# Attention: values of two key blocks and the denominators in one array visit, three banks for transposed scores, maxima placed by DMA, compact reciprocals

## The reference

```
q, k_s, v_s, k_l, v_l = heads of x@Wq, x@Wkv_short, x@Wkv_long      # 16 heads of 32
out_short = softmax(q k_s^T / sqrt(32) - |i-j|(1-decay)) v_s
out_long  = softmax(q k_l^T / sqrt(32)) v_l
out = (alpha*out_short + (1-alpha)*out_long) @ Wo
```

## Time and profile before

| | |
|---|---|
| time, median of 3 runs | 5613.65 us (5612.13 to 5614.03) |
| profiled execution, first to last instruction | 5613.5 us |
| of it attention, from the first maximum to the last mix | 641.8 to 4278.9 us |
| busy: TensorE, weight load, VectorE, ScalarE, GpSimd | 96%, 38%, 74%, 51%, 52% |
| mean granted TensorE clock | 0.981 |

### The profile page before, as it was taken

One profiled execution on the slowest core, in us unless ns is written; L12 is line 12 of the kernel. 1 busy time (PEld: TensorE's weight loads), 2 busy tenths in 40 slices (PEclk: granted clock), 3 DMA queues, 4 the chain that ended last, 5 costly groups with the idle time before them and its releaser, 6 DMA issues. The chain is left out here.

```text
span 5613.5 us, 97704 instructions
## 1 busy us (share of the span) xinstructions
PE 5382.8 (96%) x28780; PEld 2121.9 (38%) x28780; DVE 4180.9 (74%) x7218; ACT 2874.8 (51%) x5201; POOL 2933.2 (52%) x658
## 2 busy tenths in 40 slices
PE   7999899999999999999999999999996999999999
PEld 3444333333322323223233332232332555555555
DVE  5444688877877878778778787787883777777777
ACT  1111166666666666666666666666664333333332
POOL 0000088878877878778778787788884000000000
PEclk9999799999999999999999999999998999999999
DMA  4333201010101010101010101010101000000000
GB/s 135 105 104 93 81 19 33 21 29 22 33 21 29 21 34 21 29 21 33 22 29 21 34 21 29 21 33 22 29 3 49 17 22 17 22 17 22 17 22 12
DMA packets 145632, 191.62 MB, mean 34 GB/s; under 512 B 18500, under 2 KB 97988, under 8 KB 145030
## 3 DMA queue, kind: packets, MB, share of 16 engines
q1 hardware_dynamic: 145159, 185.65, 11.2%
HBM read 123.56 MB, written 61.64 MB: 33 GB/s over the span
## 5 line engine op out<-in xcount | busy, mean ns | idle before, releaser
L764 DVE TENSOR_REDUCE rowmax_parts<-scores_qk 128x1 f32<-128x512 f32 x4096 | 2569.8, 682 | 668.9 <-PE scores_qk L836 666.3
L745 ACT ACTIVATE probs_T<-scores_kq 128x512 f32<-128x512 f32 x4096 | 2263.3, 596 | 1249.5 <-PE scores_kq L836 1195.2
L704 POOL TENSOR_TENSOR probs_group_sum<-probs_T 128x2048 f32<-128x2048 f32 x384 | 1742.4, 4538 | 667.4 <-PE sums L913 395.7
L836 PE MATMUL scores_kq<-q_operand,k_operand 103*128 103x512 f16 (+3 forms) x3712 | 1279.8, 351 | 16.7 <-ACT probs_T L745 15.4
L704 POOL TENSOR_TENSOR probs_group_sum<-probs_group_sum,probs_T 128x2048 f32<-128x2048 f32 x256 | 1185.5, 4631 | 46.0 <-POOL probs_group_sum L704 45.1
L836 PE MATMUL scores_qk<-k_operand,q_operand 96*128 96x512 f16 (+4 forms) x3712 | 1178.9, 354 | 22.8 <-DMA k_operand<-positions_dram 18.5
L903 PE MATMUL outputs_T<-probs_T,v_operand 128*32 128x512 f32 x8192 | 1103.3, 611 | 52.4 <-issue 52.4
L836 PEld LDWEIGHTS scores_qk<-k_operand,q_operand 96*128 96x128 f16 (+1 forms) x3712 | 352.7, 98 | 898.6 <-DVE rowmax_parts L764 627.1
L1341 PE MATMUL f_gate_up<-w_gate_up,xq_T 128*128 128x352 f32 x2048 | 626.4, 462 | 0.8 <-issue 0.8
L836 PEld LDWEIGHTS scores_kq<-q_operand,k_operand 103*128 103x128 f16 x3712 | 361.2, 98 | 672.9 <-ACT probs_T L745 507.1
L1341 PEld LDWEIGHTS f_gate_up<-w_gate_up,xq_T 128*128 128x128 f32 x2048 | 382.5, 190 | 200.7 <-issue 2.6
(11 more groups left out here) (144 smaller groups left out, 3477.2 us busy)
## 6 DMA issues: line engine op xcount, KB each, us to landing
qk_parts_dram<-qk_parts SPq DMA_DIRECT2D x96, 256.0 KB, 2.5
q_operand<-qk_parts_dram SPq DMA_DIRECT2D x192, 128.0 KB, 2.6
k_operand<-qk_parts_dram SPq DMA_DIRECT2D x192, 128.0 KB, 2.9
v_dram<-v_heads SPq DMA_DIRECT2D x16, 1024.0 KB, 5.4
v_operand<-v_dram SPq DMA_DIRECT2D x64, 256.0 KB, 3.1
q_operand_above<-qk_parts_dram SPq DMA_DIRECT2D x96, 128.0 KB, 2.8
x_groups<-x SPq DMA_DIRECT2D x8, 1024.0 KB, 8.8
attention_dram<-o_mixed SPq DMA_DIRECT2D x128, 64.0 KB, 1.6
```

The costliest lines, as they stand in the source:

```text
L704: nc.gpsimd.tensor_tensor(total, first, probs[:, b % PBUF, :], ALU.add).then_inc(added.sem, 1)
L745: nc.scalar.activation(probs[:, kb % PBUF, qt * BANK:(qt + 1) * BANK], pb[:, k % 2, :], ACT.Exp)\
L764: nc.vector.reduce_max(rowmax[:, w % 2, c // NQ, c % NQ:c % NQ + 1], pa[:, k % 3, :], AX.X)\
L836: return nc.tensor.matmul(out, lhsT, rhs, start=start, stop=stop, skip_group_check=True)
```

## The change

TensorE's order is now in 8 steps a unit. A step has a burst (`times_v` of two key blocks, then the `count`s due at this step) and 8 slots, each with one transposed score chunk and one chunk for maxima. Transposed scores run 11 chunks ahead of the burst instead of 6 or so and have three banks (the bank that the transposes used is free). Maxima of a later unit are 20 chunks ahead instead of 16. VectorE's order follows the slots: `take` before slot 56, `invert` 16, `weigh` 32, `mix` 36; `negate` falls after slot 43's chunk.

Maxima are written as float16 into a 128 x 32 tile, turned by VectorE in 32 x 32 blocks, and put into the operand's row by four DMAs for each operand (8 in even units, 4 in odd ones). The denominators are gathered by four DMAs from one partition of 512 columns into 32 partitions of 16, inverted as one 128 x 16 reciprocal, written to DRAM by one DMA and read back by four, each spread over 32 partitions.

```diff
-ASTEPS = 12
-TURN_MAX = 12
-INVERT = 3
-WEIGH = 8
-MIX = 10
+BURST = 2
+STEPS = KB // BURST
+SLOTS = BURST * NQ
+LEAD = SLOTS + 3
+EARLY = 20
+TAKE_SUMS = 5
+INVERT = 16
+WEIGH = 32
+MIX = 36
+TAKE = (STEPS - 1) * SLOTS
-COUNT_LAG = 3
+COUNT_AT = (2, 4, 5, 7, 8, 9)
+def maximum_of(g):
+    c = (g + EARLY) % CHUNKS
+    return (1 if g + EARLY < CHUNKS else 2), c
...
-        negmax = sb("negmax", [P, 2, KB], F32)
-        maxT = sb("negmax_T", [KB, 2, P], F16)
+        negmax = sb("negmax", [P, 2, HD], F16)
+        maxT = sb("negmax_T", [P, 2, HD], F16)
+        sums_c = sb("sums_compact", [P, KB], F32)
+        inv_c = sb("inverse_compact", [P, KB], F32)
-        pb = ps("scores_kq", [P, 2, BANK], F32)
+        pb = ps("scores_kq", [P, 3, BANK], F32)
-        pt = ps("turned", [P, BANK], F32)
...
             def place_max(w, n):
-                sp.wait_ge(roundm.sem, roundm.at(n, w + 1))
+                sp.wait_ge(turned.sem, turned.at(n, w + 1))
                 for dst in (q_op[w], q_up[w]) if w % 2 == 0 else (q_op[w],):
-                    sp.dma_start(dst[MROW:MROW + 1, :], maxT[:, w % 2, :]).then_inc(maxrow[w].sem, 16)
+                    row = dst[MROW:MROW + 1, :].rearrange("o (c g j) -> o c g j", g=NQ, j=HD)
+                    for g in range(NQ):
+                        sp.dma_start(row[:, :, g, :], maxT[g * HD:g * HD + KB, w % 2, :]).then_inc(maxrow[w].sem, 16)
+            def gather_sums(w, n):
+                wait_apart(sp, sums_out, sums_out.at(n, w + 1), passed)
+                wait_apart(sp, inverted, inverted.at(n, w), passed)
+                for qt in range(NQ):
+                    sp.dma_start(sums_c[qt * HD:(qt + 1) * HD, :], sums[qt * HD:qt * HD + 1, :].rearrange("o (r e) -> o r e", e=KB))\
+                        .then_inc(gathered.sem, 16)
+            def spread_inverse(w, n):
+                wait_apart(sp, inverted, inverted.at(n, w + 1), passed)
+                sp.dma_start(inv_scr[w % 2:w % 2 + 1, :].rearrange("o (p e) -> (o p) e", e=KB), inv_c[:, :])\
+                    .then_inc(inv_out.sem, 16)
+                wait_apart(sp, inv_out, inv_out.at(n, w + 1), passed)
+                wait_apart(sp, weighed, weighed.at(n, w), passed)
+                for qt in range(NQ):
+                    sp.dma_start(inv[qt * HD:(qt + 1) * HD, :],
+                                 inv_scr[w % 2:w % 2 + 1, qt * BANK:(qt + 1) * BANK].to_broadcast([HD, BANK]))\
+                        .then_inc(inv_in.sem, 16)
...
                 for w in range(UNITS):
+                    back = unit_before(w, n, first)
+                    if back:
+                        gather_sums(*back)
+                        spread_inverse(*back)
+                        if back[0] % 2:
+                            store(back[0] // 2, back[1])
                     if after(w, n, last):
                         place_max(*after(w, n, last))
-                    if w == 0 and not first:
-                        store(1, n - 1)
-                    if w == 2:
-                        store(0, n)
...
-            def round_max(w, n):
...
             def take_sums(w, n):
                 act.wait_ge(counted.sem, counted.at(n, (w + 1) * GROUPS_N))
-                act.wait_ge(weighed.sem, weighed.at(n, w))
+                act.wait_ge(gathered.sem, gathered.at(n, w * NQ))
...
             def negate(w, n):
                 dve.wait_ge(maxed.sem, maxed.at(n, (w + 1) * (CHUNKS + 1) - 1))
-                nc.vector.tensor_reduce(negmax[:, w % 2, :], rowmax[:, w % 2, :, :], AX.X, ALU.max, negate=True)\
+                nc.vector.tensor_reduce(negmax[:, w % 2, 0:KB], rowmax[:, w % 2, :, :], AX.X, ALU.max, negate=True)\
                     .then_inc(maxed.sem, 1)
+                dve.wait_ge(maxed.sem, maxed.at(n, (w + 1) * (CHUNKS + 1)))
...
+                nc.vector.transpose(maxT[:, w % 2, :], negmax[:, w % 2, :]).then_inc(turned.sem, 1)
...
-            def invert(w, n, r):
-                dve.wait_ge(sums_out.sem, sums_out.at(n, w + 1))
-                nc.vector.reciprocal(inv[:, r * P:(r + 1) * P], sums[:, r * P:(r + 1) * P]).then_inc(inverted.sem, 1)
+            def invert(w, n):
+                dve.wait_ge(gathered.sem, gathered.at(n, (w + 1) * NQ))
+                dve.wait_ge(inv_out.sem, inv_out.at(n, w))
+                nc.vector.reciprocal(inv_c[:, :], sums_c[:, :]).then_inc(inverted.sem, 1)
...
+                    for g in range(CHUNKS):
+                        if g == TAKE:
                             take(w, n)
+                        if back and g == INVERT:
+                            invert(*back)
+                        if back and g == WEIGH:
                             weigh(*back)
+                        if back and g == MIX and back[0] % 2:
+                            mix(back[0] // 2, back[1])
+                        distance, c = maximum_of(g)
                         unit = after(w, n, last, distance)
+                        if unit:
                             max_chunk(*unit, c)
                             if c == CHUNKS - 1:
                                 negate(*unit)
...
-            def turn_max(w, n):
...
+                    pe.wait_ge(expd.sem, expd.at(n, number - 2))
-                bank = pb[:, number % 2, :]
+                bank = pb[:, number % 3, :]
...
+                    for j in range(STEPS):
+                        for kb in range(BURST * j, BURST * (j + 1)):
+                            times_v(w, n, kb)
+                        for u, behind in (((w, n), 0), (back, STEPS)):
+                            for g in range(GROUPS_N):
+                                if u and COUNT_AT[g] == j + behind:
+                                    count(*u, g)
+                        for s in range(SLOTS):
+                            b = j * SLOTS + s + LEAD
+                            if b < CHUNKS:
+                                scores_for_exp(w, n, b)
+                            elif ahead:
+                                scores_for_exp(*ahead, b - CHUNKS)
+                            distance, c = maximum_of(j * SLOTS + s)
+                            unit = after(w, n, last, distance)
                             if unit:
+                                scores_for_max(*unit, c)
```

More of the change, by code:

```diff
@@ L529, in adds_until, with last_with @@
     return sum(max(0, sum(b <= max(kb, g[1]) for b in g) - 1) for g in GROUPS if g[0] <= kb)
-def chunks_of(i):
-    k = (i - ASTEPS) % KB * NQ
-    return (1 if i < ASTEPS else 2), list(range(k, k + NQ))
-EARLY = (KB - ASTEPS) * NQ
+def maximum_of(g):
+    c = (g + EARLY) % CHUNKS
+    return (1 if g + EARLY < CHUNKS else 2), c
+def last_with(k, ring, total):
+    return max(m for m in range(total) if m % ring == k)
 ROW_LOADS = UNITS + 6 * UNITS // 2
@@ L731, in one_pass @@
                     for kb in range(KB):
-                        if back and kb == COUNT_LAG + 1:
+                        if back and kb == TAKE_SUMS:
                             take_sums(*back)
-                        if kb == (TURN_MAX + 2) % KB and after(w, n, last):
-                            round_max(*after(w, n, last))
                         old = w * KB + kb - PBUF
@@ L755, in _ @@
         def _(dve):
+            nc.vector.memset(negmax[:, :, :], 0.0)
             for w in (1, 3):
@@ L802, in one_pass @@
                 for w in range(UNITS):
-                    ahead, back = after(w, n, last), unit_before(w, n, first)
-                    for i in range(KB):
-                        if i == KB - 1:
+                    back = unit_before(w, n, first)
+                    for g in range(CHUNKS):
+                        if g == TAKE:
                             take(w, n)
-                        if back and INVERT <= i < INVERT + NQ:
-                            invert(*back, i - INVERT)
-                        if back and i == WEIGH:
+                        if back and g == INVERT:
+                            invert(*back)
+                        if back and g == WEIGH:
                             weigh(*back)
-                        distance, chunks = chunks_of(i)
+                        if back and g == MIX and back[0] % 2:
+                            mix(back[0] // 2, back[1])
+                        distance, c = maximum_of(g)
                         unit = after(w, n, last, distance)
-                        for c in chunks if unit else ():
+                        if unit:
                             max_chunk(*unit, c)
@@ L816, in one_pass @@
                                 negate(*unit)
-                        if back and i == MIX and back[0] % 2:
-                            mix(back[0] // 2, back[1])
             one_pass(0, True, False)
@@ L824, in _ @@
             end = (UNITS - 1, PASSES - 1)
-            for r in range(NQ):
-                invert(*end, r)
+            invert(*end)
             weigh(*end)
@@ L928, in one_pass @@
                     ahead, back = after(w, n, last), unit_before(w, n, first)
```

(32 more changed lines are left out.)

60 lines of the change are left out of this document (33 added, 27 removed).

## The result

| | before | after |
|---|---|---|
| median, same chip | 5613.42 us (4 runs) | 5851.66 us (4 runs, the lowest 5850.01) |
| profiled execution, first to last instruction | 5613.5 us | 5850.6 us |
| mean granted TensorE clock | 0.981 | 0.968 |

The ratio is 1.0424, with a 95% interval of 1.0407 to 1.0441: 238 us slower. The forecast was slower by 115 us (5728), with a range that ended at 5786. One of the four runs after took 7741.39 us at a granted clock of 0.647; the ratio leaves it out, and the other three lie between 5850.01 and 5852.63.

A forecast was written before the change was run, and what follows sets the result against it. TensorE was held by the ring of three score banks, waiting for VectorE's maxima. A pass of 231.4 us against 224.0, over some 15.5 passes, gave +115, ends +3: 5731, stated as 5728 us, range 5562 to 5786.

The forecast's parts named there:

- The stretch between bursts is 16 score matmuls with the same three banks for maxima: Between bursts, VectorE's chain of reductions sets the pace: 4.09 us a stretch, 32.7 a unit against 32.4 before.
- the forecast's plain unit: A unit summed without contention: 54.5 us against 54.4 before, including 0.35 for the mix of every second unit.
- they miss: Second rival: weighing and mix miss GpSimd's adds, other terms as taken; 5607 us, no measurable change, chance 0.15.
- the collision: Two-input VectorE steps (weighing, mix) block until GpSimd's running add ends; 8.0 us a pass in all.
- price of 1.7: The weighing, asked for in the middle of the sixth add, delays the reductions by 1.7 us a unit.
- The first rival: Weighing and mix miss the adds and the bursts gain: a pass of 220.6, 5563 us, chance 0.26.
- Price 1.7 in every second unit: The mix, asked for during the seventh add, takes 2.4 us instead of 0.7.
- escapes: After a boundary, the weighing is asked for near the sixth add's end and costs nothing; the mix pays some 1.2.
- the boundary, 5.4: Pass boundary: 5.4 us instead of 6.4, as full banks and a burst cover the 1.0 ScalarE's pause costs TensorE.
- late maxima, 0.15 a unit: In even units the eighth maxima DMA lands 0.6 us late; the ring swallows most, leaving 0.15 on average.
- the third rival: Maxima land 2.3 us late as well: 58 us more, 5786, chance 0.12; sign: their waits not under 20 us.
- the end: After the loop, gathering and spreading the sums in place of four reciprocals: +6 us.

The follow-up runs named there:

- e9: e1 with each of VectorE's maxima taken over 256 of the 512 columns of a bank: 5438.88 us, ratio 0.9678.
- e10: e6 with each of VectorE's maxima taken over 256 of the 512 columns of a bank: 5492.76 us, ratio 0.9777.
- e1: The changed kernel with weighing and mix both moved to slot 56, and maxima ahead of the store on SP's queue: 5612.05 us, ratio 0.9995.
- e2: e1 with the weighing back at slot 32, so only the mix is at slot 56: 5721.36 us, ratio 1.0190.
- e7: e1 with the maxima of a later unit 24 chunks ahead instead of 20: 5563.34 us, ratio 0.9911.
- e6: The changed kernel with visits of one key block instead of bursts of two, and weighing and mix at slot 56: 5514.13 us, ratio 0.9822.

## Why the prediction was wrong, point by point

**Right: what bounds the new order.** "The stretch between bursts is 16 score matmuls with the same three banks for maxima": 4.09 forecast, 4.10 to 4.16 measured; bursts 1.88 and 2.76 against 1.86 and 2.71. e9 and e10 show the cause and not only the number: with a faster VectorE the stretches between bursts fall, and those of single visits stay. The sum is less sound than it looks. In e1 the mix is off the path, so the forecast's plain unit is 54.5-0.35 = 54.15 there; 54.39 and 53.99 were measured. But e1's nearness to 5607 ("they miss", 5 us) is in part luck: with the mix hidden, 22 us less, the forecast is 5585, and most of the 27 us that it is short by is the boundary.

**Right: that the collision decides, and where it lies.** The phases are those of the forecast (1.51 and 2.91 us into the sixth and seventh add, forecast 1.4 and 2.9), and the weighing takes 3.6 us instead of 0.75. Its price of 1.7 fits as a mean (1.71); a pass pays 7.0 for weighings and not 5.1. The first rival (missed, 5563), the second (5607) and their 0.41 fell with the two rows of o_weighed.

**Wrong: "Price 1.7 in every second unit", for the mix.** This is the step of the forecast that failed. It priced the stand of VectorE and took the work of TensorE behind it at its usual speed. But the stretch with both steps is 8.2 us long for 16 score matmuls, TensorE stands 2.5 us at its end, and the burst behind it runs at a granted clock of 0.52 instead of 1.00. From e2 to after, a pass is 8.8 us longer. The forecast had 1.7 and 1.2 for the mixes and 2x0.7 for their own time, 4.3. Of the 4.5 us that are missing, 3.6 are the two bursts of 4.79 and 4.20 us where 2.71 is usual; over 15.5 passes that is 55 us. The earlier trace rows had shown a visit at half clock behind a stand, and I used it to size a pass of the array, not to ask where else TensorE would come to stand. This is the largest term of the miss.

**Wrong: the unit after a boundary "escapes".** Its stretch with the weighing takes 8.24 as in w=2. It was to pay nothing for the weighing and 1.2 for the mix; it paid 6.2 with the mix's own 0.7 (64.58 against e1's 58.37). The slow burst 0 delays GpSimd's first add as well, since the add waits for the sums of that burst: it starts 0.42 us behind the burst in w=0, much as in the other units (0.44), the sixth add starts 30.8 us after the beginning of burst 0 instead of 26.3, and the weighing falls 1.5 us into it in all four units.

Together: e1 to after, the four units differ by 6.2, 1.5, 5.6 and 2.5, which is 15.7 a pass. Without the mixes' own 1.4 that is 14.3 where the forecast had 8.0. These 6.3 us are the larger part of the 7.9 (15.3 against 7.4) by which the pass grew more than forecast, which is the 124 us between 5728 and 5852. The forecast's own terms add up to 5731; why it says 5728 is not told.

**Wrong in size: the boundary, 5.4.** In e1 units w=0 and w=3 exceed w=2 and w=1 by 4.4 and 3.6, 7.9 together; in the kernel before it is 7.4. The forecast had the third bank and the longer burst cover ScalarE's pause and save 1.0; nothing was saved, and 0.5 was added, which is 1.5 of the 7.9 us. In both kernels the profile puts TensorE's stand down to "issue" and not to ScalarE: 52.4 us in 13 waits before, 66.7 in 26 after (two at a jump). That ScalarE's pause costs TensorE 1.0 was read into the earlier trace rows. Nor is it the length of the burst (7.3 us against 2.71): single visits pay 10.1 by unit lengths, and before, too, the granted clock is 0.50 for 6.3 us behind the stand. Why a jump costs a little more or less in one order than in another stays open.

**Wrong in size, small: late maxima, 0.15 a unit.** The stretch ahead of burst 7 shows 0.87 more than 4.10 in w=1 and 0.53 in w=3. The waits for the tile sum to 30 us, not 10. The forecast had named 20 us as the limit beyond which the third rival holds, and by that sign it does; by the time lost it does not. e7, which takes these waits away, wins 1.3 us a pass in the stretches ahead of burst 7, 20 us in all, where the rival had 58 and the forecast 10.

**Right: the end.** From the last sums' copy to the last mix 10.4 us against 4.9, forecast +6.

**Not forecast at all: that bursts lose.** I took them as neutral (54.5 against 54.4) against the old order, where sums had visits of their own. Against single visits that hold the sums they cost 98 us, or 49 with the maxima turned earlier (e7): VectorE idles through each burst, and it can work ahead only as far as its banks reach. What e6 gains on the kernel before fits the visits of sums that it merges and the third bank for transposed scores, but neither was run by itself; which of them holds how much stays open. The earlier trace rows had only the waits for VectorE, 776 us. The same view has almost as much for ScalarE in the kernel before, which the forecast mentions without its size:

```profile
PEld scores_kq L836 <- ACT probs_T L745: 696.2, 1073, 2.0
```

In e6 the waits for VectorE have fallen to 115 us, though its reductions are no faster, and those for ScalarE are 616. So the ring of three score banks may not be all that held the old order; no run takes the two rings apart.

## What to carry to other kernels

Before a two-input VectorE step from SBUF is moved in a kernel in which GpSimd adds, write out in which add it lands: in the kernel before, one block later was worth 200 us for a step of 0.77 us. Price a stall by what TensorE does next as well: where the granted clock fell in the stand, a burst of 2.71 us took up to 5.3. Longer visits for one engine only pay if the other engine isn't the one that sets the pace between them: with bursts the kernel lost 98 us, and with half the reductions' columns it won 54.

## What the runs showed of the hardware that was not expected

- The granted clock fell within a stand of 2.52 us, at the end of a stretch of 6.00 us in which TensorE worked 2.61 us; stretches of 5.6 us for the same 16 matmuls left it at 1.00 (every burst behind them took 2.71).
- A VectorE step with two SBUF inputs ends 0.54 to 0.62 us after the GpSimd add that it fell into, wherever it was asked for: durations of 1.8, 2.6, 3.6, 4.55, 4.8 and 4.96 us for steps of 0.7 and 0.75. The Trainium skill, "SBUF — State Buffer", Who interferes with whom, says that who issued first decides who is blocked. The traces agree for the VectorE side (the add keeps its 4.54 us); the add of 2028.01 above, which began while a blocked weighing was ending, took 4.96.
- A loop's jump costs 9 to 11 us in these kernels, with bursts and with single visits: TensorE stands 4 to 5 us, and the work behind the stand runs at the lower clock (7.3 us for a burst of 2.71 in e1).
- A reduction of 256 columns takes 0.43 us, of 512 columns 0.68: half of the columns save only a third. The 32x32 transpose of 128x32 float16 took 0.21, the 128x16 reciprocal 0.24, against 0.94 for one of 128x128.
